# A decoder layer on one core: the 56 groups of matmuls whose results are not read are left out

## What is computed

```python
x = layernorm(x + attn(x, Wq, bq, Wk, bk, Wv, bv, Wo, bo))      # causal, 1024 keys
x = layernorm(x + xattn(x, ctx, ctx, mask, w_q, w_k, w_v, w_o)) # 64 context keys
x = layernorm(x + ffn(x, w_gate, w_up, w_down))                 # 256 -> 1024 -> 256

# attn: softmax(q k^T / 4, causal) v, then Wo and bo
# ffn:  bitlinear(silu(bitlinear(x, w_gate)) * bitlinear(x, w_up), w_down), where bitlinear
#       rounds the rows of x to 8 bits and the weights to -1, 0, 1 times a scale
```

## Time and profile before

| | |
|---|---|
| median of 3 runs | 835.85 us (834.56 to 835.97) |
| span of the profiled execution | 833.7 us; its own time with what lies around the span is not given, the median is 2.15 us above the span |
| PE, matmuls | 782.8 us busy (94%), 7699 records |
| DVE | 683.1 us (82%) |
| ACT | 575.6 us (69%) |
| POOL | 348.9 us (42%) |
| L812 | 31.5 us of PE's busy time, 224 matmuls |
| chain that ended last | PE 57%, DVE 23%, ACT 6%, issue 6%, POOL 5%, DMA 1% |

### The profile page before, as it was taken

How to read it: one execution, slowest core, us unless ns; L and a number is a source line. 1 busy time by engine, 2 the same in 40 slices (tenths; PEclk the granted TensorE clock), 3 DMA queues, 4 the chain that set the end, 5 groups by cost and what they waited for, 6 DMA issues and landing times.

```text
span 833.7 us, 20715 instructions
## 1 busy us (share of the span) xinstructions
PE 782.8 (94%) x7699; PEld 390.2 (47%) x7726; DVE 683.1 (82%) x1254; ACT 575.6 (69%) x753; POOL 348.9 (42%) x587
## 2 busy tenths in 40 slices
PE   9789999999999999999999999999999989999985
PEld 6434444354553434534454444543545443445644
DVE  6899998678987799877999689884899858836698
ACT  2467865558856598655885769857697579964595
POOL 5763355334433245522534334443524403551335
PEclk9999999999999999999999999999999999999999
DMA  6433003100201011011122010111000000010001
GB/s 187 128 108 102 2 21 88 26 18 15 82 17 45 1 29 50 16 45 42 36 65 66 12 29 21 42 40 30 9 21 30 18 2 26 3 51 2 2 1 53
DMA packets 37238, 32.89 MB, mean 39 GB/s; under 512 B 9829, under 2 KB 33349, under 8 KB 37141
## 3 DMA queue, kind: packets, MB, share of 16 engines
q1 hardware_dynamic: 33796, 28.89, 12.4%
q0 software_dynamic: 1440, 1.48, 0.8%
q10 hardware_dynamic: 1904, 1.18, 0.6%
HBM read 14.55 MB, written 4.19 MB: 22 GB/s over the span
## 4 chain that ended last, share of the span: by engine, by line
PE 57%; DVE 23%; ACT 6%; issue 6%; POOL 5%; DMA 1%; ACTq 0%; SPq 0%; POOLq 0%; DVEq 0%
DVE shift L1432 10%; PE ps L1067 9%; PE ps L848 8%; PE ps L1052 6%; PE ps L1030 6%; PE ps L861 5%; PE ps L928 3%; DVE amax L1384 3%; PE ps L1013 2%; POOL xt L787 2%; ACT probs L1173 2%; PE ps L958 2%; PE ps L970 2%; DVE stats L1344 2%; PE ps L953 2%
## 5 line engine op out<-in xcount | busy, mean ns | idle before, releaser
L1173 ACT ACTIVATE probs<-ps 128x1024 f32<-128x1024 f32 (+3 forms) x384 | 294.2, 810 | 121.4 <-PE ps L1052 119.4
L1432 DVE TENSOR_REDUCE shift<-ps 128x2 f32<-128x1024 f32 (+2 forms) x320 | 343.2, 1111 | 38.4 <-PE ps L1030 21.8
L1067 PE MATMUL ps<-probs,v_aug 128*32 128x512 f32 (+3 forms) x1536 | 156.9, 498 | 0.1
L727 POOL TENSOR_SCALAR_AFFINE_SELECT probs<-probs 128x512 f32<-128x512 f32 x128 | 80.8, 640 | 163.0 <-ACT probs L1173 162.1
L1052 PE MATMUL ps<-q_stack,k_stack 49*128 49x512 f16 (+3 forms) x768 | 115.2, 328 | 11.5 <-ACT probs L1173 4.6
L1030 PE MATMUL ps<-k_stack,q_stack 48*128 48x512 f16 (+3 forms) x768 | 114.8, 328 | 11.3 <-DVE shift L1432 6.4
L1052 PEld LDWEIGHTS ps<-q_stack,k_stack 49*128 49x128 f16 x768 | 38.9, 93 | 110.2 <-ACT probs L1173 41.8
L1030 PEld LDWEIGHTS ps<-k_stack,q_stack 48*128 48x128 f16 x768 | 41.1, 93 | 94.6 <-ACT probs L1173 29.5
L1036 PEld LDWEIGHTS ps<-causal,pick_h 64*128 64x128 bf16 x1024 | 46.7, 95 | 13.9 <-issue 0.4
L1036 PE MATMUL ps<-causal,pick_h 64*128 64x64 bf16 x1024 | 53.1, 189 | 0.0
L1067 PEld LDWEIGHTS ps<-probs,v_aug 128*32 128x32 f32 x1536 | 35.2, 108 | 37.5 <-issue 27.2
(11 more groups left out here) (241 smaller groups left out, 1369.2 us busy)
## 6 DMA issues: line engine op xcount, KB each, us to landing
q_stack<-part_sb SPq DMA_DIRECT2D x164, 32.0 KB, 2.0
k_stack<-part_sb SPq DMA_DIRECT2D x147, 32.0 KB, 2.0
xT<-in_x_cols SPq DMA_DIRECT2D x8, 512.0 KB, 4.5
xt<-in_x SPq DMA_DIRECT2D x8, 512.0 KB, 3.9
out_x<-xt SPq DMA_DIRECT2D x7, 512.0 KB, 3.0
q_stack<-shiftT SPq DMA_DIRECT2D x128, 1.0 KB
k_stack<-part_sb POOLq DMA_DIRECT2D x45, 32.0 KB, 2.0
region<-in_w_gate SPq DMA_DIRECT2D x4, 256.0 KB, 3.4
```

The costliest lines, as they stand in the source:

```text
L727: pool.affine_select(out=blk, in_=blk, compare_op=ALU.is_ge, fill=0.0, base=0, pattern=[[0, HG], [1, P]], channel_multiplier=-1).then_inc( ...
L1067: mm = pe.matmul(ps[DV * i:DV * (i + 1), SUM_BANK, off:BANK], v_aug[:, kb, at:at + DV], probs_of(b, n)[:, i, :], start=first, stop=last)
L1173: act.activation(probs_of(b, n)[:, 2 * p:2 * p + 2, :], pair(u)[:, :, 0:BANK - off], ACT.Exp, scale=exp_scale).then_inc(probs_ready, 1)
L1432: dve.tensor_reduce(to[:, :, pairs[0]:pairs[-1] + 1, qb % TH], pair(u)[:, :, 0:len(pairs) * w].rearrange("p j (h w) -> p j h w", w=w), AX. ...
```

## The change

`STIRS` becomes 0, and the 56 entries `z` with their bank digits go from `ORDER`. Nothing else stands elsewhere in the string; since the string is broken into lines of 108 characters, all its lines read otherwise. Two of them, and the constant:

```diff
-STIRS = 56
+STIRS = 0
...
-    "a45z6m23a45m01aa45m23fffoa01m45afm23a01z6sgm45a01az6m23m01wwm45om23r6m45m01fa23oosa23aa45gz6m23m01o45r6sm23m"
+    "a45m23a45m01aa45m23fffoa01m45afm23a01sgm45a01am23m01wwm45om23r6m45m01fa23oosa23aa45gm23m01o45r6sm23m01oa23aa"
...
-    "23v1v0vhuz6z6z6ttvt"
+    "4v23v1v0vhuttvt"
```

More of the change, by code:

```diff
@@ L51 @@
     "rr6r0r1ssr2r3r6r0sgsggr6swm01m23m45m01m23m45r6ffm23m45m01m23r6ffgm01a45m23r6a01am45w2w3w6ca45a01aoa45a23am01"
-    "a45z6m23a45m01aa45m23fffoa01m45afm23a01z6sgm45a01az6m23m01wwm45om23r6m45m01fa23oosa23aa45gz6m23m01o45r6sm23m"
-    "01oa23aa45a23m01om45a23m01oom45oa23z6z6m01o23a45oa01m23z6m45a01m23ffoa45m01fz6xga23xm45a01aoa23m45m01a23m45o"
-    "wm23m01aa45oa23m45aw6a01oa01aa23m45m01z6m45m23woooa01z6z6a45o23a01oa45m23a01om45a23a01om23a45z6m01z6m45m23wz"
-    "6a01z6z6aa45a23az6rz6a45a01aa23oa01am45m23a01oa45m01aoa23m45r6a01aa23oooa01am45a23gz6z6o01m23m45r6m23m01rr4a"
@@ L56 @@
[L56 to L85, removed]
@@ L86 @@
-    "h3oooohh2h6o45h3eh2u45v01z3h6bu3uuh05v4u23vvh01h24u6h01h23h45uu6u0uv23h45u6u1h23v0u1h23vu05v4v2h3vv2v6u04v6h"
-    "2hv05u23v05u23z4z4u01v23u01hhhz6v23v45hhu6uuv45z2h23v6h2h3h4vh6uvuuvh5h0h1h2h3h4z6z6uu56hhhhh4z0z3h3u5u4u6vh"
-    "hhhvu3u5u2h01h6h5z4vv45uuhhhhh23h6h4h5uuu0u6v4v1v5v0hhhhuv4v6h23h5uuuu01vh23z6vvvv6v5vu01z4h4h5hu6u0uvvvv45v"
-    "23v1v0vhuz6z6z6ttvt"
+    "a45m23a45m01aa45m23fffoa01m45afm23a01sgm45a01am23m01wwm45om23r6m45m01fa23oosa23aa45gm23m01o45r6sm23m01oa23aa"
+    "45a23m01om45a23m01oom45oa23m01o23a45oa01m23m45a01m23ffoa45m01fxga23xm45a01aoa23m45m01a23m45owm23m01aa45oa23m"
@@ new lines @@
+    "45aw6a01oa01aa23m45m01m45m23woooa01a45o23a01oa45m23a01om45a23a01om23a45m01m45m23wa01aa45a23ara45a01aa23oa01a"
+    "m45m23a01oa45m01aoa23m45r6a01aa23oooa01am45a23go01m23m45r6m23m01rr4a23m56ara01oa23m45m01oaa23ooom45a23m01m23"
+    "m45awa01r6egga01o23aa45oem01m45a23oaa01m23ooom45m01a23rr6o01ra23m45obm01p23a01a45m23p6m45m23a01p6ppa23a01m45"
+    "r6m01m23om01a45op23m01m45m01m23p6m01a45m23p6pp4p5p2p3paoa45a01p6p2p3p4aa56a01oaa23a56aa01p4oa23p04a23grr6rp0"
+    "1p24m01r6p01p23p45m01p45a23p01m23m01p45ogrm23oom45m01p6p4a01a23bo56oa01ppm45r6m01a23m45oa01m23pa45oaa01m23pa"
@@ new lines @@
+    "45paopa45m01ra23r6m45aa23p01om23a01aa45p6p0p1m45m23ooom45gm23op0p1p6p4p0p1p5pa23ar4a01pppp5p6o01a45aa23poa45"
+    "m01gpppp23p6r4aa01a56am23a01a45p6poaa01a23papm45pp01p6p2p3pm01xa45a23par6m23xpgpa45a01aop45m01p6p23m45m01oop"
+    "6p4o23a01a56ooa01ppm23p45ooom01m23m45p6a23m01p4a01a23po56oa01opa23m01m45ooa01m23p45m01m23m45tp6m23m01a45p6m4"
+    "5paa01a23p6p0p1p4paa23a56om23aa01a56ap4a01p5a23p6p4om01a23p6a45oop02rr6r4op01p24p01rr6p23o45p01oa45p01p23oa0"
+    "1m45p23m01m45p6a01m45m23rp6pa45a01a23aom45om01m23a45om45a01m23ppaa01a45aa01a23aa45pa01gam23oom45m23gpa01r6m4"
@@ new lines @@
+    "5m01pa23aop45m23m01a45p6m23m45p0p1p6m23gm01rm45op6p2p3p0p6o12a45p3ar0ra45a23appppp1p6m45pa23a01pppooooom01m4"
+    "5aa23r6o01p23p4rp6ga01aa23a45apeoa23a01am45m23pppp01p6p4p5pa01a23oooom01m45pppp23p6o01om23p45p6bm01a23a45p6p"
+    "pp0p1a45a23p6p45com23m45a01p6p4a01a23r6pm01pa23am45om01m23a45oa01p45om01m23aa45p6m01m45m23p6pp4a01p5aa23p6a0"
+    "1p4paa23m01oa45m23a01p6p4p5a23ooop6a01a23ro45tp6om45gp02m45om45p01p24r6rp01p23p45m01a23p45p01a23m45p01m23m45"
+    "oa01m23p6m01p4pm23a01aa56r4m01a56opaa23m45a01apora01a23aea45a01am23pppoom45m01a23r6a45m23bgp01om45m23m01p6r4"
@@ new lines @@
+    "aom23m01p6p4p5p2p6xm34gm01p5p2p3p4a56o01ooa01apa23a45apppp6p0a23a45appppr6m23p01p4p6oooa23pm45a01gr6po01ppp2"
+    "3p4p6p5paa23a01aoa23a45aa01m23m45poppp01p6m23m45p01p6m23a01p4ppxp56ooa23m01gm45p6a01m23op4a23o01a56oa01pm23p"
+    "a45om01ra45a23aoa01a45om23p01m45m23m01p6m23m45m01p6pp2aa45p3p6p0pa45aa12om45a23p6aa01tep2p3a45op6a01a45m23p6"
+    "ooom01r2p35o01br2rp45p02p45r6ra01ggp23p45m23a01op45a23p01a45m23p01oa23a45m01p6am45m01p2a45a01ar6pm01m45m23oa"
+    "01poa01aa45a23paa01a45apm23oa01a45am23oa01ppm45m23m01rr6rm23m45p01oom23oa01p6gm45p0p1m23m45p6p0p1o23p6p0p1aa"
@@ new lines @@
+    "23m45p6oa45m01aa23a45aoa01a23ppppp6p4oooaa01a23ppm56r4ppo01p23p5p6oaa45a01aa23a45gppppp01p6p2p3pa45oooom01pp"
+    "pp23p6m45o01om23p45p6m01a23a45p6pptep0p1a23a45rp6p23om45a23a01p6a23am01m45p6ppa01a23aoa01a45om01aa23a45oam45"
+    "a23m01r6m01p23m45oa01a23p6m01a23m45p6m23a45m01opop6p4op5p2pro01gr3p6p2p5p4a01oa23m01a56rp4oa23p05a23ar4p01p2"
+    "5p01gop01a23p45m01a23aop45p01a23m45m23p01om45m01p6p4ba01aa23a56aoa01ppa23am45rr6a45a23m01ooocam45a01a23ppr6a"
+    "a23a45appo01m23a45oom01m23p45m01oom23oa45p6o01m23p4m01p5m23p6p4p5m01p6p4m23aa56p0p4m23a01poaa45a01aa23a45app"
@@ new lines @@
+    "pp6p2pa45a01pooom45m23a01r6oa45m23ppp01p6p4a23a01go56oa23a45ppppp01p6p2p3poa45a23om01m45ppaopp23m01p6a45m23p"
+    "01p6a45m23aa01p6ppa45p01aa23om45m01a23p6ap4pm01pa23a56ar4a23a56aom01a23om45a23aoom01p23o45om23m45a01p6m23tm0"
+    "1p4pp6p5a23aa01p4p6m23pa01aa45op6a01p2p3ap4a56a01aa56m23a01p4ooom23p04o23om23p01p24p01goop01aa23p45m01ooa23p"
+    "45p01a23o45p01oa45a01a23p6p0ppa23a45om01a23a45aa23m01a45apopa01a45aa23oa01m45m23m01ppoaa45a23om01p45om23a01m"
+    "45p6m23p0p1om45p6p2om45m01p3p6p2p4p5pa01a34o56pppp2op0m56a34a12oa34ppppp56p0p1m23poea01a45apppp23p6p0p1pa45o"
@@ L90 @@
+    "a01apppm23op45p6a23a01aop45p6a01a23p4ph6h5aa23a01h4h23oooa01ba23h5ph4ha23ha01to56oa23oa01a23a45ooaa23h01a45o"
+    "aa23a01ah6a01a23h4hah6h5h2h3oooohh2h6o45h3eh2u45v01h6bu3uuh05v4u23vvh01h24u6h01h23h45uu6u0uv23h45u6u1h23v0u1"
+    "h23vu05v4v2h3vv2v6u04v6h2hv05u23v05u23u01v23u01hhhv23v45hhu6uuv45h23v6h2h3h4vh6uvuuvh5h0h1h2h3h4uu56hhhhh4h3"
+    "u5u4u6vhhhhvu3u5u2h01h6h5vv45uuhhhhh23h6h4h5uuu0u6v4v1v5v0hhhhuv4v6h23h5uuuu01vh23vvvv6v5vu01h4h5hu6u0uvvvv4"
+    "5v23v1v0vhuttvt"
 )
```

## The result

The kernel with the change has a median of 841.07 us in seven runs (837.33 to 848.81), the kernel before 835.65 us in seven beside it (834.35 to 836.89). The ratio is 1.0068, with a 95% interval of 1.0046 to 1.0089: slower by 0.7%. A second session of eleven runs gave 839.93 us against 835.49 us, ratio 1.0065 (1.0033 to 1.0096).

The account below looks back on a forecast made before the run. TensorE, busy 94%, was not taken as the bound everywhere: DVE or waits limit many places. Time given back, -1.3 us, plus clock falls, +3.4 us, gave +2.1 us: 835.85 to 838.0 us, range 834.1 to 841.8 us.

Parts of the forecast that it names:

- the chain's 13.5 us: Filler matmuls' time on the chain that ended last, mostly between 60 and 180 us; at most 13.5 us gain.
- Step 1: At the units' 38 places, waits follow nearly all; three units' worth given back, 1.3 us gain, ends 0 and 13.5.
- Step 2: Clock falls behind thin stretches at 94, 173, 781, perhaps 749 us; four new falls at 0.85 us, 3.4 us loss.
- the ceiling of 1.7 us: In any 3.4 us clock fall TensorE does half its work, so it costs at most 1.7 us.
- The clock holds: Rival: clock stays up everywhere without units, only 1.3 us given back, 834.6 us; chance 0.25.
- The filler was in the way: Rival: units on the chain delayed ACT and DVE all along; 13.5 us back, 829.1 us even with four falls; chance 0.13.
- Many falls: Rival: thin stretches all over 40 to 140 us fall too, ten falls in all, 843.1 us; chance 0.08.

Follow-up runs that it names:

- the first trace: Profiled execution of the changed kernel, all 56 units removed from the kernel before, in the first session; 837.33 us, span 835.6 us.

## Why the prediction was right

**Direction and mechanism held, and most of the places.** It forecast 838.0 us and slower; measured were 841.07 us in the first session and 839.9 us over all 18 runs, inside 834.1 to 841.8. New falls came behind 94, 173 and 749 us, where it looked for them, but not behind 781, and several came elsewhere. The reading that chain time of filler is a ceiling was right: of the chain's 13.5 us at most 4.9 came back, by the bound above. The test that it set for itself, that TensorE's idle time grows by most of 24.6 us, came out at 23.9 us.

**Step 1, TensorE's time given back,** was put at 1.3 us, three units' worth, by choice. The traces show 1.0 and 0.9 us for 43 of the 56 units, so for these the choice was about right, and so was the reading that nothing is gained where DVE is full: from 41.9 to 54.9 us the first trace gains 0.2 us. What the other 13 units gave back, and with it the whole, stays open between 1 us and the 4.9 us of the bound; the two lines put it at 3.3 us, one common slope at 1.2 us.

**Step 2, the clock, was too small, mostly in the number of falls.** The number was four new ones; the runs show 31.1 - 9.8 = 21.3 us more at 1.2 GHz, about six stretches of 3.4 us, of which a part may lie behind TensorE's last matmul. I looked for places that must fall and not at how many others might: keeping 12 of the 56 units brought back less than half of the slowing, and the profiled execution, the fastest of seven, shows fewer falls than the average run. The price of a fall was taken as 0.85 us for 3.4 us; the traces show about 1.0 us, the line of the changed kernel 0.366 x 3.4 = 1.25 us. Halving the ceiling of 1.7 us was a choice, and a little too kind: at 752.5 us the whole ceiling was paid.

So the sum, +2.1 us against +5.4 us in the first session, was short. It lies inside the range because that allowed for seven falls and no gain.

**The rivals.** *The clock holds*: refuted by the windows. The first rule of the Trainium skill cited there (TensorE: Matmul & The Clock Gate, "Why this matters for your kernels"), a gap between bursts, fails again: at 684.2:687.6 TensorE was busy 2.32 of 3.40 us ahead of a fall, in short bits. Its second ("A second HAM failure mode: psum-queue depth-cycling" on the same page), short idle bits between groups, fits. *The filler was in the way*: needed 5.1 us given back; the bound allows 4.9, and the traces show 1.0 us for 43 of the units. *Many falls*: some runs are of this kind, 848.8 to 849.0 us at a clock of 0.969.

## What to carry to other kernels

An engine's idle time costs nothing on its own, but on TensorE it can cost the clock: ahead of removing work that "computes nothing", look at the granted clock behind thin stretches. Here a fall of 3.4 us cost 1.0 us by the traces and 1.25 us by the line, and 1.7 us where TensorE alone was on the chain. The filler is cheap where it is put into waits that exist: two whole-array matmuls in each unit did what four did, and both more in each (851 us) and fewer units (838 us) were worse. Judge such a change by the clocks of ten runs and not by one profile, because the same program loses its clock at different places in each execution. And before a lead between two traces is put down to a change, look whether it was there ahead of the first instruction that the change touches.

## What was not expected of the hardware

Time in use alone is not what keeps the clock: matmuls of 32 rows, 268 ns each, left the mean clock at 0.989 where those of 128 rows, 273 ns each, gave 0.994. Filler of bf16 transposes gave 0.994 and no filler 0.982, although the Trainium skill (TensorE: Matmul & The Clock Gate, Part 4) says that a transpose doesn't count as busy in the way that a matmul does; in this case's runs it did. And a stretch of TensorE's use that looks alike in two executions, 2.40 and 2.39 us of 3.40 at 378.3, was followed by a fall in one and by full clock in the other.
